# Four graph layers on one core: the norm's row product over 128 rows, the last graph's scores by two heads, and another order of every engine's list

## The chip, the core and the metric

One core of a Trainium2 chip runs one program. The metric is the device time of that program in microseconds (us). The core has five engines, each with an instruction queue of its own: TensorE (PE, products and transposes into PSUM), VectorE (DVE), ScalarE (ACT), GpSimd (POOL) and SyncE (SP, which here only issues DMAs). They are held together by semaphores that each instruction raises and waits for.

## What is computed

The input is `x` of 16 x 512 x 256 and `adj` of 16 x 512 x 512: 16 graphs of 512 nodes with 256 features. Four layers follow each other, each as `x = x + layer(relu(layernorm(x)), adj)`:

```
L0: xw = h @ W1.T; m = Be * (H.T @ xw); z = relu(Dn * (H @ m) + b1)     # H = adj != 0
    z = layer_norm(z) * gamma + beta; the same conv with W2, b2; + h
L1: e = leaky_relu(sj[j] + si[i] + ab); t = rows of adj * exp(e), divided by their sums
    relu(h @ Wk[0] + (t @ h) @ Wk[1] + (t @ t @ h) @ Wk[2] + bk)
L2: per head of 32 features: xp = h @ Wp + bp; xc = xp @ C.T
    att = tanh(adj * (xc @ xp.T)); relu(att @ xp)
L3: relu((adj @ h) @ kernel) * (row of h is not all zero)
```

## The kernel before

**Tiles.** A graph is four row tiles of 128 nodes. The weights stay in SBUF. Where float32 accuracy is wanted, an operand is split into a high part (type fp32r) and a low one, and a product is made of three: high by high, high by low, low by high (`three`, or two where one side is exact). The low parts come from DVE or POOL by a subtraction, the high ones mostly from ACT. PSUM is cut into three banks `ring_f`, handed round among the steps of layers 0 and 1, two double banks `ring_b` for the scores and the rest of layers 2 and 3, and `pv_acc`, in which the attends accumulate.

**Steps.** Each engine has a function of its own for each step, and one name on several engines is one step. Layers 0 and 1 are the f_ steps: `bn`, `variance`, `p_rstd` (POOL), `offset` and `f_h0` make a norm (k = 0 to 4 in their argument: H0, Z, H1, H2, H3); `f_H` and `f_HT` make the incidence matrix and its transpose from `adj_n` and `adj_t`, `f_dn` the node weights; then `f_m`, `f_u`, `f_conv1`, relu, `f_zT` (transposes), `f_stat`, `f_xw`, `f_m2`, `f_y`. In `f_hT`, `f_sj`, `f_q`, `f_max`, `f_mask`, `f_exp`, `f_sums`, `f_trans`, `f_tt`, `f_r1`, `f_r`, `f_x1` and `f_x2` the attention hop follows. Layers 2 and 3 are the k_ steps: `k_hT`, `k_xp`, `k_xc`, `k_xn`, then eight units (two halves of the heads by four row tiles). In each, PE makes four heads' scores in twelve 32-row products (`k_scores`, S0 to S7 below), DVE multiplies them by `at`, two heads at a time (`k_unit`, the gating), ACT takes tanh, two heads at a time, and PE multiplies with `xp_n` (`k_attend`, A0 to A7). `k_outT` transposes the result back and DVE adds it to `xb`; `k_ax` and `k_out` are layer 3; `k_y` on POOL adds the last sum before the store. `k_keep` and `k_xh` are copies on ACT.

**The row product.** The norm inside layer 0 is not applied to z itself. `xw` (line 1440) multiplies the raw z by the weights, and one product more adds the means and biases: `stat_t` rows 0 to 5 by `rowz` rows 0 to 5. It is the first of the group for each of four output tiles. `sel` by `rowb` does the like elsewhere, with 128 rows that are zero but for a few.

**Order.** Each engine's order is written out by hand as three lists: `first` (graphs 0 to 4), `turn` (a hardware loop) and `last`. `all_turns` (line 354) runs them; the loop goes from 5 to 15, so it has ten turns. An entry `(d, step, ...)` in `turn` is that step for the graph b - d: the engine works on graph b's layers 0 and 1 while it works on graph b-2's units and b-1's k_xp. In `first` the first number is the graph itself, in `last` it counts from the end (-1 is graph 15). Nothing but these lists and the semaphores sets what comes after what: an engine that waits holds back all that is behind in its list. SP's list (line 462) holds the loads (`next_adjt`, `next_adj`, `next_x`, ...) with the waits that say when their tile is free. `ends(g)` (line 191) is true for graph 15 in `last`, `apart(g)` for graph 14 there; these two use other banks for some steps, so that graph 14's `k_ax` and `k_out` may stand anywhere beside graph 15's scores.

**Waits that matter.** `k_scores` of unit u waits until both halves of unit u - 1 are gated (`gated`, line 1636), since it writes the same two banks; `k_attend` waits for both tanh of its unit. `f_m` 0 waits for all four low parts of h0, which POOL makes (`f_h0`, line 503). `k_xp` waits for the low part of `k_hT`. `k_outT` on DVE adds into `xb` and `k_outT` on PE waits for the copies `k_xh`. The last graph's `k_scores` 0 waits for its three inputs and for DVE's `k_outT` of graph 14.

## Time and profile before

| | |
|---|---|
| median of 3 runs | 1603.48 us (1602.44 to 1604.51) |
| the profiled execution | 1603.98 us, span 1602.0 us, mean granted clock 0.983 |
| PE busy | 1476.8 us, 92% |
| DVE busy | 1192.0 us, 74% |
| ACT busy | 886.4 us, 55% |
| POOL busy | 285.6 us, 18% |
| HBM traffic | 57 GB/s over the span |

How to read it: a share of busy time is an average over the fill at the start, twelve or so full turns and the tail. PE's busy time includes time at which one product waits for another inside PE, since the ends of its products are modelled. A granted clock of 1.00 is the upper of TensorE's two levels, 2.4 GHz. One row of the timeline can hold several instructions of one kind (x12), and the bracket at its end is the idle time before it, with the instruction that ended it.

### The profile page before, as it was taken

What the parts mean: (1) busy time and instruction counts of PE and PEld (TensorE: products, weight loads), DVE (VectorE), ACT (ScalarE), POOL (GpSimd) and SP (SyncE); (2) the same over time, 40 slices, a digit from 0 to 9 for tenths busy, and PEclk for the clock granted to TensorE, in tenths of its full rate; (3) what the DMA queues carried; (4) which work ended last, traced back from release to release, by engine and by line L of the source; (5) the groups of instructions that cost most, each with busy time, mean ns of one, the idle gap of its engine ahead of it and who ended that gap; (6) DMA issues with size and microseconds to landing.
All of it is one profiled execution on the core that took longest, in us unless ns stands there. A gap on an engine that the chain in (4) does not pass through costs nothing.

```text
span 1602.0 us, 28213 instructions
## 1 busy us (share of the span) xinstructions
PE 1476.8 (92%) x10426; PEld 1117.6 (70%) x10426; DVE 1192.0 (74%) x2667; ACT 886.4 (55%) x1501; POOL 285.6 (18%) x348
## 2 busy tenths in 40 slices
...
DMA packets 58554, 92.21 MB, mean 58 GB/s; under 512 B 4289, under 2 KB 23297, under 8 KB 58497
## 3 DMA queue, kind: packets, MB, share of 16 engines
...
## 4 chain that ended last, share of the span: by engine, by line
PE 65%; issue 16%; DVE 10%; ACT 5%; POOL 2%; DMA 1%; ACTq 0%; POOLq 0%; SPq 0%; DVEq 0%
PE ring_f L1360 41%; PE ring_b L1360 9%; PE ring_b L1640 6%; PE pv_acc L1656 6%; PE ring_f L1537 2%; POOL rstd L501 2%; ACT hf L580 1%; DVE att L1191 1%; DVE m L992 1%; ACT uz L570 1%; DVE bns L951 1%; DVE tr_l L992 1%; DVE uz L992 1%; PE ring_f L1437 1%; DVE rows L1119 1%
## 5 line engine op out<-in xcount | busy, mean ns | idle before, releaser
L1191 DVE TENSOR_TENSOR att<-ring_b,at 128x1024 f32<-128x1024 f32 x256 | 308.2, 1219 | 93.5 <-PE ring_b L1640 89.0
L728 ACT ACTIVATE att<-att 128x1024 f32<-128x1024 f32 x256 | 268.3, 1055 | 163.8 <-DVE att L1191 162.5
L501 POOL TENSOR_TENSOR rstd<-var,mhalf 128x4 f32<-128x4 f32 x80 | 81.7, 1021 | 735.4 <-DVE var L966 735.3
L1360 PE MATMUL ring_f<-w,uz 128*128 128x256 f32 (+1 forms) x896 | 197.0, 342 | 2.4 <-DVE uz L992 1.8
L1360 PE MATMUL ring_f<-m,tr_h 128*128 128x256 f32 x1024 | 190.8, 287 | 0.0
L1360 PEld LDWEIGHTS ring_f<-w,uz 128*128 128x128 f32 x896 | 150.7, 191 | 34.7 <-DVE uz L992 7.5
L1360 PEld LDWEIGHTS ring_f<-m,tr_h 128*128 128x128 f32 x1024 | 158.6, 191 | 22.8 <-issue 22.0
L1360 PEld LDWEIGHTS ring_f<-m,inc_n 128*128 128x128 f32 x1024 | 129.2, 197 | 37.0 <-issue 26.6
L1360 PE MATMUL ring_f<-m,inc_n 128*128 128x256 f32 x1024 | 136.3, 291 | 16.3 <-POOL m L505 16.2
L1360 PE MATMUL ring_f<-m,tr_l 128*128 128x256 f32 x512 | 144.5, 282 | 0.0
L1656 PE MATMUL pv_acc<-att,xp_n 128*32 128x512 f32 x1024 | 134.9, 604 | 4.6 <-ACT att L728 3.5
L1640 PE MATMUL ring_b<-xc_t,xp_s 32*128 32x512 f32 x1536 | 125.4, 427 | 13.0 <-ACT xp_n L570 5.6
L1360 PE MATMUL ring_b<-at,h 128*128 128x512 f32 x240 | 109.4, 600 | 5.8 <-ACT h L580 5.8
L575 ACT ACTIVATE m<-ring_f,be 128x256 fp32r<-128x256 f32 x128 | 53.7, 473 | 107.4 <-PE ring_f L1360 106.9
L1640 PEld LDWEIGHTS ring_b<-xc_t,xp_s 32*128 32x128 f32 x1536 | 64.4, 184 | 65.3 <-issue 34.7
L1360 PE MATMUL ring_f<-wk,uz 128*128 128x256 f32 x768 | 103.4, 284 | 0.0
L570 ACT ACTIVATE uz<-ring_f 128x512 fp32r<-128x512 f32 x128 | 71.6, 597 | 51.6 <-PE ring_f L1360 23.5
L1360 PEld LDWEIGHTS ring_f<-wk,uz 128*128 128x128 f32 x768 | 96.8, 190 | 2.5 <-issue 2.0
L1360 PEld LDWEIGHTS ring_f<-m,tr_l 128*128 128x128 f32 x512 | 97.9, 191 | 0.0
L520 POOL TENSOR_TENSOR h<-h,xb 128x256 f32<-128x256 f32 x64 | 47.4, 756 | 276.2 <-ACT h L756 276.2
L997 DVE SCALAR_TENSOR_TENSOR m<-ring_f,be,m 128x256 fp32r<-128x256 f32 x128 | 55.5, 477 | 43.1 <-ACT m L575 42.7
L505 POOL TENSOR_TENSOR m<-hf,m 128x256 fp32r<-128x256 f32 x64 | 53.0, 852 | 183.6 <-DVE m L1050 183.6
...
## 6 DMA issues: line engine op xcount, KB each, us to landing
...
```

The lines of the kernel that those rows point to most:

```text
L501: pool.tensor_tensor(rstd[k][:], var[k][:], mhalf[:], ALU.pow).then_inc(rstd_made[k].sem, 1)
L505: pool.tensor_tensor(m1[:, 1, i], hf[:, i], m1[:, 0, i].bitcast(F32), ALU.subtract).then_inc(h0_lo.sem, 1)
L520: pool.tensor_tensor(y_part[:, i], y_part[:, i], xb[:, i], ALU.add).then_inc(y_made.sem, 1)
L570: act.activation(dst, src, ACT.Copy).then_inc(made.sem, 1)
L575: ins = act.activation(dst_of(t), tile[:, i * D:(i + 1) * D], ACT.Copy, scale=by[:, t:t + 1])
L728: act.activation(v, v, ACT.Tanh).then_inc(tanh_made.sem, 1)
L992: dve.tensor_tensor(dst, src, hi.bitcast(F32), ALU.subtract).then_inc(made.sem, 1)
L997: ins = dve.scalar_tensor_tensor(dst_of(t), tile[:, i * D:(i + 1) * D], by[:, t:t + 1], hi_of(t).bitcast(F32), ALU.mult, ALU.subtract)
L1191: dve.tensor_tensor(att[:, u % 2, 2 * half:2 * half + 2], ring_b[half][:], at[:, u % NT].unsqueeze(1).broadcast_to([P, 2, N]), ALU.mult).t ...
L1360: ins = pe.matmul(dst, lhsT, rhs, start=(first and n == 0), stop=(last and n == len(pairs) - 1), skip_group_check=True)
L1640: ins = pe.matmul(ring_b[h // 2][:, h % 2], xp_s[head, p, part, t * P:(t + 1) * P], xc_t[head, c, part], start=(n == 0), stop=(n == 2), sk ...
L1656: ins = pe.matmul(pv_acc[h * KH:(h + 1) * KH, :], xp_n[:, t, ch:ch + KH], att[:, u % 2, h], start=(t == 0), stop=(t == NT - 1), skip_group ...
```

## The change

Four things change. `stat_t` and `rowz` are cleared whole in `set_up_w2` (two memsets more, and the counts SET_W2 and SET_DONE two higher), and `xw` then takes all 128 rows of both in its first product. For the last graph `k_scores` makes two heads at a time: three products for each of heads 0 and 1, behind the gating of the first half of the unit before, then the same for heads 2 and 3 behind the second half. All five engines have other lists for the loop. And `first` and `last` are other lists as well: `first` repeats the order of the loop from graph 1 on, and in `last` graph 14's `k_ax` and `k_out` stand ahead of the last graph's `k_scores` 0 on PE, ACT and DVE, and ACT's `k_keep` for the last graph moves from behind unit 7 into unit 3. The lists are shown for one loop turn: whole for POOL, SP and PE (old and new), the new one for DVE, and the head and the end of the new one for ACT; the old ones are in the code above. Of `last`, PE's end is shown, old and new.

```diff
@@ -340,7 +340,7 @@
-        SET_W1, SET_COLUMNS, SET_W2, SET_DONE = 1, 12, 24, 42
+        SET_W1, SET_COLUMNS, SET_W2, SET_DONE = 1, 12, 26, 44
@@ -461,21 +461,21 @@
             def turn(b):
                 run_turn(b, G, (
-                    (0, next_x), (2, next_at), (4, store), (3, next_at2), (0, next_adj), (0, next_wrow),
+                    (0, next_x), (3, next_at2), (0, next_wrow), (2, next_at), (4, store), (0, next_adj),
                     (0, next_adjt),
                 ))
 
...
@@ -521,27 +521,27 @@
             def turn(b):
                 run_turn(b, G, (
-                    (0, p_rstd, 0), (0, f_h0, 0), (0, f_h0, 1), (3, k_y, 1), (3, k_y, 2), (0, f_h0, 2),
-                    (0, f_h0, 3), (3, k_y, 3), (0, f_sum, 0), (1, p_rstd, 3), (0, f_sum, 1), (0, f_sum, 2),
-                    (0, f_sum, 3), (0, p_rstd, 1), (0, p_rstd, 2), (2, p_rstd, 4), (2, k_y, 0),
+                    (0, p_rstd, 0), (0, f_h0, 0), (3, k_y, 1), (3, k_y, 2), (3, k_y, 3), (0, f_h0, 1),
+                    (0, f_h0, 2), (0, f_h0, 3), (0, f_sum, 0), (0, f_sum, 1), (0, f_sum, 2), (0, f_sum, 3),
+                    (1, p_rstd, 3), (0, p_rstd, 1), (0, p_rstd, 2), (2, p_rstd, 4), (2, k_y, 0),
                 ))
...
@@ -759,19 +759,19 @@
+                    (0, f_h0, 0), (2, k_unit, 2, 0), (1, f_r, 1), (0, f_h0, 1), (0, f_h0, 2), (2, k_unit, 2, 1),
+                    (0, f_h0, 3), (2, k_unit, 3, 0), (2, k_keep), (2, k_unit, 3, 1), (0, f_m, 0), (0, f_m, 1),
+                    (2, k_xh, 0), (2, k_unit, 4, 0), (0, f_u, 0), (0, f_u, 1), (0, f_relu, 0), (2, k_unit, 4, 1),
+                    (0, f_relu, 1), (2, k_unit, 5, 0), (0, f_relu, 2), (0, f_relu, 3), (0, f_zT, 0), (0, f_zT, 1),
+                    (0, f_zT, 2), (1, k_h2, 0), (1, k_h2, 1), (0, f_zT, 3), (2, k_unit, 5, 1), (1, k_h2, 2),
+                    (1, k_h2, 3), (0, f_stat), (2, k_unit, 6, 0), (0, f_xw, 0), (0, f_xw, 1), (2, k_unit, 6, 1),
...
+                    (2, k_out, 1), (0, f_tt, 0), (0, f_tt, 1), (0, f_tt, 2), (0, f_tt, 3), (1, k_unit, 0, 0),
+                    (1, k_unit, 0, 1), (0, f_r, 0), (1, k_unit, 1, 0), (1, k_unit, 1, 1),
...
@@ -900,7 +899,9 @@
                 step(dve.memset(sel[:].bitcast(F32), 0.0))
-                step(dve.memset(rowb[:].bitcast(F32), 0.0), now=True)
+                step(dve.memset(rowb[:].bitcast(F32), 0.0))
+                step(dve.memset(stat_t[:].bitcast(F32), 0.0))
+                step(dve.memset(rowz[:].bitcast(F32), 0.0), now=True)
@@ -1211,145 +1212,144 @@
+                    (0, bn, 0, 0), (3, bn, 4, 2), (3, bn, 4, 3), (3, variance, 4), (3, offset, 4), (1, f_hT, 0),
+                    (1, f_hT, 1), (0, bn, 0, 1), (2, k_xc), (1, f_q, 0), (1, f_q, 1), (0, bn, 0, 2), (1, f_max, 0),
+                    (1, f_mask, 0), (3, k_mask), (1, f_q, 2), (1, f_max, 1), (1, f_q, 3), (1, f_mask, 1),
+                    (1, f_max, 2), (3, k_ax, 0), (1, f_mask, 2), (1, f_max, 3), (1, f_mask, 3), (3, k_ax, 1),
+                    (2, k_split, 0), (1, f_sums), (1, f_trans, 0), (1, f_trans, 1), (1, f_trans, 2),
+                    (1, f_trans, 3), (2, k_split, 1), (1, f_tt, 0), (1, f_tt, 1), (0, bn, 0, 3), (1, f_tt, 2),
+                    (1, f_tt, 3), (2, k_unit, 0, 0), (2, k_unit, 0, 1), (0, f_HT, 0), (2, k_unit, 1, 0),
+                    (0, variance, 0), (0, f_HT, 1), (2, k_unit, 1, 1), (1, f_r, 0), (0, f_HT, 2), (0, offset, 0),
+                    (0, f_HT, 3), (2, k_unit, 2, 0), (2, k_unit, 2, 1), (1, f_r, 1), (0, f_H), (0, f_be),
+                    (2, k_unit, 3, 0), (0, f_h0), (0, f_dn, 0), (2, k_unit, 3, 1), (0, f_dn, 1), (2, k_unit, 4, 0),
+                    (2, k_unit, 4, 1), (1, f_x2, 0), (1, f_x2, 1), (0, f_dn, 2), (0, f_dn, 3), (1, bn, 3, 0),
+                    (1, bn, 3, 1), (0, f_m, 0), (1, bn, 3, 2), (0, f_m, 1), (0, f_dn2), (1, bn, 3, 3),
+                    (1, variance, 3), (0, f_u, 0), (0, f_u, 1), (2, k_unit, 5, 0), (0, f_conv1, 0),
+                    (0, f_conv1, 1), (2, k_unit, 5, 1), (0, f_conv1, 2), (0, f_conv1, 3), (0, bn, 1, 0),
+                    (0, bn, 1, 1), (1, offset, 3), (0, bn, 1, 2), (0, f_zT, 0), (0, f_zT, 1), (0, bn, 1, 3),
+                    (0, f_zT, 2), (0, variance, 1), (0, f_zT, 3), (0, f_stat), (2, k_unit, 6, 0),
+                    (2, k_unit, 6, 1), (0, f_xw, 0), (2, k_unit, 7, 0), (0, f_xw, 1), (2, k_unit, 7, 1),
+                    (0, f_m2, 0), (0, f_m2, 1), (1, k_hT), (2, k_outT, 0), (2, k_outT, 1), (0, f_y, 0),
+                    (0, f_y, 1), (0, bn, 2, 0), (0, bn, 2, 1), (0, bn, 2, 2), (0, bn, 2, 3), (0, variance, 2),
+                    (2, bn, 4, 0), (2, bn, 4, 1), (0, offset, 2),
...
@@ -1440,7 +1440,7 @@
                 zh, zl = (a[:].rearrange("p a n -> p (a n)") for a in (uz, m2))
                 for i in (2 * q, 2 * q + 1):
-                    pairs = [(stat_t[0:6, i * P:(i + 1) * P], rowz[0:6])] if ks[-1] == HT_ - 1 else []
+                    pairs = [(stat_t[:, i * P:(i + 1) * P], rowz[:])] if ks[-1] == HT_ - 1 else []
@@ -1632,15 +1632,18 @@
-                else:
+                elif not ends(g):
                     pe.wait_ge(gated.sem, gated.after(g, 2 * u))
-                for n, (p, c) in enumerate(((0, 0), (0, 1), (1, 0))):
-                    for h in range(4):
-                        head = slice(h * KH, (h + 1) * KH)
-                        ins = pe.matmul(ring_b[h // 2][:, h % 2], xp_s[head, p, part, t * P:(t + 1) * P],
-                                        xc_t[head, c, part], start=(n == 0), stop=(n == 2), skip_group_check=True)
-                        if n == 2 and h % 2 == 1:
-                            ins.then_inc(scored.sem, 1)
+                for heads in (((0, 1), (2, 3)) if ends(g) else ((0, 1, 2, 3),)):
+                    if ends(g) and u > 0:
+                        pe.wait_ge(gated.sem, gated.after(g, 2 * u - 1 + heads[0] // 2))
+                    for n, (p, c) in enumerate(((0, 0), (0, 1), (1, 0))):
+                        for h in heads:
+                            head = slice(h * KH, (h + 1) * KH)
+                            ins = pe.matmul(ring_b[h // 2][:, h % 2], xp_s[head, p, part, t * P:(t + 1) * P],
+                                            xc_t[head, c, part], start=(n == 0), stop=(n == 2), skip_group_check=True)
+                            if n == 2 and h % 2 == 1:
+                                ins.then_inc(scored.sem, 1)
@@ -1698,18 +1701,18 @@
-                    (0, f_m, 0), (2, k_scores, 3), (1, f_x2, 1), (2, k_attend, 2), (0, f_m, 1), (2, k_scores, 4),
-                    (0, f_u, 0), (2, k_attend, 3), (0, f_u, 1), (2, k_scores, 5), (0, f_conv1, 0), (0, f_conv1, 1),
-                    (0, f_conv1, 2), (0, f_conv1, 3), (2, k_attend, 4), (2, k_scores, 6), (0, f_zT, 0),
-                    (0, f_zT, 1), (2, k_attend, 5), (0, f_zT, 2), (0, f_zT, 3), (0, f_xw, 0), (0, f_xw, 1),
-                    (0, f_stat), (2, k_scores, 7), (0, f_xw, 2), (0, f_xw, 3), (2, k_attend, 6), (0, f_m2, 0),
-                    (0, f_m2, 1), (1, k_hT), (2, k_outT, 0), (0, f_y, 0), (2, k_attend, 7), (0, f_y, 1),
-                    (2, k_outT, 1), (1, k_xp, 0), (1, k_xp, 1), (1, k_xc, 0), (1, k_xc, 1), (1, k_xn, 0),
-                    (0, f_hT, 0), (0, f_hT, 1), (1, k_xn, 1), (0, f_sj), (0, f_q, 0), (0, f_q, 1), (2, k_ax, 0, 0),
-                    (0, f_q, 2), (0, f_q, 3), (2, k_ax, 0, 1), (2, k_ax, 1, 0), (2, k_ax, 1, 1), (2, k_out, 0),
-                    (2, k_out, 1), (0, f_tt, 0), (0, f_tt, 1), (0, f_tt, 2), (1, k_scores, 0), (0, f_tt, 3),
-                    (0, f_r1), (0, f_r, 0), (1, k_scores, 1), (0, f_r, 1), (0, f_x1), (1, k_attend, 0),
-                    (1, k_scores, 2), (1, k_attend, 1), (0, f_x2, 0),
+                    (0, f_m, 0), (0, f_m, 1), (2, k_attend, 3), (0, f_u, 0), (0, f_u, 1), (2, k_scores, 5),
+                    (0, f_conv1, 0), (0, f_conv1, 1), (0, f_conv1, 2), (0, f_conv1, 3), (2, k_attend, 4),
+                    (0, f_zT, 0), (0, f_zT, 1), (2, k_scores, 6), (0, f_zT, 2), (0, f_zT, 3), (0, f_xw, 0),
+                    (0, f_xw, 1), (0, f_stat), (2, k_attend, 5), (0, f_xw, 2), (2, k_scores, 7), (0, f_xw, 3),
+                    (0, f_m2, 0), (1, k_hT), (0, f_m2, 1), (2, k_attend, 6), (2, k_attend, 7), (0, f_y, 0),
+                    (2, k_outT, 0), (2, k_outT, 1), (0, f_y, 1), (1, k_xp, 0), (1, k_xp, 1), (1, k_xc, 0),
+                    (1, k_xc, 1), (1, k_xn, 0), (1, k_xn, 1), (0, f_hT, 0), (0, f_hT, 1), (0, f_sj), (0, f_q, 0),
+                    (0, f_q, 1), (2, k_ax, 0, 0), (0, f_q, 2), (0, f_q, 3), (2, k_ax, 0, 1), (2, k_ax, 1, 0),
+                    (2, k_ax, 1, 1), (2, k_out, 0), (2, k_out, 1), (0, f_tt, 0), (0, f_tt, 1), (0, f_tt, 2),
+                    (1, k_scores, 0), (0, f_tt, 3), (0, f_r1), (0, f_r, 0), (1, k_scores, 1), (0, f_r, 1),
+                    (1, k_attend, 0), (1, k_scores, 2), (0, f_x1), (1, k_attend, 1), (1, k_scores, 3),
+                    (0, f_x2, 0), (1, k_attend, 2), (1, k_scores, 4), (0, f_x2, 1),
...
-                (-2, k_attend, 6), (-2, k_attend, 7), (-2, k_outT, 0), (-2, k_outT, 1), (-1, k_xp, 0),
-                (-1, k_xp, 1), (-1, k_xc, 0), (-1, k_xc, 1), (-1, k_xn, 0), (-1, k_xn, 1), (-1, k_scores, 0),
-                (-2, k_ax, 0, 0), (-1, k_scores, 1), (-2, k_ax, 0, 1), (-1, k_attend, 0), (-1, k_scores, 2),
-                (-2, k_ax, 1, 0), (-1, k_attend, 1), (-1, k_scores, 3), (-2, k_ax, 1, 1), (-1, k_attend, 2),
-                (-1, k_scores, 4), (-1, k_attend, 3), (-1, k_scores, 5), (-2, k_out, 0), (-1, k_attend, 4),
-                (-1, k_scores, 6), (-2, k_out, 1), (-1, k_attend, 5), (-1, k_scores, 7), (-1, k_attend, 6),
-                (-1, k_attend, 7), (-1, k_outT, 0), (-1, k_outT, 1), (-1, k_ax, 0, 0), (-1, k_ax, 0, 1),
...
+                (-2, k_outT, 1), (-1, k_xp, 0), (-1, k_xp, 1), (-1, k_xc, 0), (-1, k_xc, 1), (-1, k_xn, 0),
+                (-1, k_xn, 1), (-2, k_ax, 0, 0), (-2, k_ax, 0, 1), (-2, k_ax, 1, 0), (-2, k_ax, 1, 1),
+                (-2, k_out, 0), (-2, k_out, 1), (-1, k_scores, 0), (-1, k_scores, 1), (-1, k_attend, 0),
+                (-1, k_scores, 2), (-1, k_attend, 1), (-1, k_scores, 3), (-1, k_attend, 2), (-1, k_scores, 4),
+                (-1, k_attend, 3), (-1, k_scores, 5), (-1, k_attend, 4), (-1, k_scores, 6), (-1, k_attend, 5),
+                (-1, k_scores, 7), (-1, k_attend, 6), (-1, k_attend, 7), (-1, k_outT, 0), (-1, k_outT, 1),
+                (-1, k_ax, 0, 0), (-1, k_ax, 0, 1), (-1, k_ax, 1, 0), (-1, k_ax, 1, 1), (-1, k_out, 0),
+                (-1, k_out, 1),
             )
```

## Rows read from the trace of the kernel before

**Rows 1.** the profile's page, part 1: busy time, share of the span, instructions
```profile
PE 1476.8 (92%) x10426; PEld 1117.6 (70%) x10426; DVE 1192.0 (74%) x2667; ACT 886.4 (55%) x1501; POOL 285.6 (18%) x348
```

**Rows 2.** one turn: stretch, us, PE, PEld, DVE, ACT, POOL busy, PEclk, DMA, GB/s
```profile
670.00:764.00 94.00, 90.64 (x652) 68.56 (x651) 72.70 (x165) 54.66 (x94) 17.60 (x21) 1.00 0.18 59
```

**Rows 3.** PE timeline, f_m 0 of graphs 2, 5, 8: start, us, operation
```profile
199.67 3.52 PE L1360 MATMUL ring_f<-m,inc_n 128*128 128x256 f32 x28
...
481.65 2.08 PE L1360 MATMUL ring_f<-m,inc_n 128*128 128x256 f32 x16
...
764.07 2.08 PE L1360 MATMUL ring_f<-m,inc_n 128*128 128x256 f32 x16
```

**Rows 4.** waits of PE from 670 to 764: who waits <- for whom
```profile
PE ring_b L1360 <- DVE tr_l L992: 1.4, 1, 1.4
```

**Rows 5.** PE timeline around k_xp and f_sj of that turn
```profile
716.78 0.60 PE L1664 MATMUL ring_b<-ident,xh_t 128*128 128x128 f32 x4
718.58 3.06 PE L1360 MATMUL ring_b<-tr_l,wp 128*128 128x512 f32 x12 [1.20 <-DVE xb L1199]
...
726.21 1.63 PE L1360 MATMUL ring_f<-uz,v 128*128 128x512 f32 x6 [0.63 <-DVE uz L992]
```

**Rows 6.** PE timeline, scores and ax in the last graph's stretch
```profile
1544.71 0.98 PE L1640 MATMUL ring_b<-xc_t,xp_s 32*128 32x512 f32 x12 [1.56 <-DVE xc_t L992]
1545.68 1.95 PE L1360 MATMUL ring_f<-at,h 128*128 128x512 f32 x4
...
1566.64 0.98 PE L1640 MATMUL ring_b<-xc_t,xp_s 32*128 32x512 f32 x12
...
1570.14 0.98 PE L1640 MATMUL ring_b<-xc_t,xp_s 32*128 32x512 f32 x12
```

**Rows 7.** DVE timeline, gating of the last graph's unit 7
```profile
1571.21 2.36 DVE L1191 TENSOR_TENSOR att<-ring_b,at 128x1024 f32<-128x1024 f32 x2 [1.14 <-PE ring_b L1640]
```

**Rows 8.** PE timeline, row products and the change from scores to products
```profile
702.95 0.38 PE L1360 MATMUL ring_f<-rowz,stat_t 6*128 6x256 f32 x1
...
703.82 0.38 PE L1360 MATMUL ring_f<-rowz,stat_t 6*128 6x256 f32 x1
...
750.94 0.97 PE L1640 MATMUL ring_b<-xc_t,xp_s 32*128 32x512 f32 x12
751.84 0.50 PE L1360 MATMUL ring_f<-m,tr_h 128*128 128x256 f32 x2
...
754.81 0.28 PE L1360 MATMUL ring_f<-rowb,sel 128*128 128x256 f32 x1
...
755.64 0.28 PE L1360 MATMUL ring_f<-rowb,sel 128*128 128x256 f32 x1
```

**Rows 9.** DVE timeline, k_outT 1 and a bn of H3 behind f_y
```profile
717.84 0.68 DVE L1199 SCALAR_TENSOR_TENSOR xb<-ring_b,xb 128x512 f32<-128x512 f32 x1
...
719.75 0.41 DVE L951 BATCH_NORM_STATS2 bns<-xb 128x6 f32<-128x256 f32 x1
```

**Rows 10.** PE timeline, transposes of f_zT
```profile
787.60 1.09 PE L1437 MATMUL ring_f<-ident,rows 128*128 128x128 f32 x8
```

**Rows 11.** ACT timeline, the last relus of that turn
```profile
786.22 1.37 ACT L618 ACTIVATE rows<-rows 128x512 f32<-128x512 f32 x2
```

**Rows 12.** SP timeline: the load of adjT; then its time to landing
```profile
745.09 0.37 SPq L375 DMA_DIRECT2D rows<-in_adjT  x1
...
DMA to landing us min/median/max: 5.9/6.1/6.4
```

**Rows 13.** POOL timeline, an addition in graph 0 and two f_h0 in the loop
```profile
16.05 1.17 POOL L514 TENSOR_TENSOR xf<-x_in,hf 128x256 f32<-128x256 f32 x1
...
757.92 1.80 POOL L505 TENSOR_TENSOR m<-hf,m 128x256 fp32r<-128x256 f32 x2 [9.78 <-DVE m L1050]
```

**Rows 14.** groups by line, the set-up: busy us, mean ns, idle before
```profile
L903 DVE MEMSET rowb<- 128x256 f32 x1 | 0.3, 272 | 0.0
```

**Rows 15.** ACT timeline, ACT's xc copy of the last graph
```profile
1542.38 1.03 ACT L570 ACTIVATE xc_t<-ring_b 128x1024 fp32r<-128x1024 f32 x1 [1.27 <-PE ring_b L1360]
```

More of the change, by code:

```diff
@@ L1308, in _ @@
[L1308 to L1311 removed]
+                (0, bn, 0, 0), (0, bn, 0, 1), (0, bn, 0, 2), (0, bn, 0, 3), (0, f_HT, 0), (0, variance, 0),
@@ new lines, in _ @@
+                (0, f_HT, 1), (0, f_HT, 2), (0, offset, 0), (0, f_HT, 3), (0, f_H), (0, f_be), (0, f_h0),
+                (0, f_dn, 0), (0, f_dn, 1), (0, f_dn, 2), (0, f_dn, 3), (0, f_m, 0), (0, f_m, 1), (0, f_dn2),
+                (0, f_u, 0), (0, f_u, 1), (0, f_conv1, 0), (0, f_conv1, 1), (0, f_conv1, 2), (0, f_conv1, 3),
+                (0, bn, 1, 0), (0, bn, 1, 1), (0, bn, 1, 2), (0, f_zT, 0), (0, f_zT, 1), (0, bn, 1, 3),
+                (0, f_zT, 2), (0, variance, 1), (0, f_zT, 3), (0, f_stat), (0, f_xw, 0), (0, f_xw, 1),
@@ L1312, in _ @@
+                (4, f_xw, 1), (2, k_unit, 7, 1), (4, f_m2, 0), (4, f_m2, 1), (3, k_hT), (2, k_outT, 0),
+                (2, k_outT, 1), (4, f_y, 0), (4, f_y, 1), (4, bn, 2, 0), (4, bn, 2, 1), (4, bn, 2, 2),
+                (4, bn, 2, 3), (4, variance, 2), (2, bn, 4, 0), (2, bn, 4, 1), (4, offset, 2),
             )
             last = (
[L1314 to L1315 removed]
```

527 lines of the change are left out of this document (243 added, 284 removed).

## The prediction

> **What bounds the kernel now.** I read the page first. TensorE (PE) is busy for 92% of the span [rows 1], so a reordering alone can win at most what PE does not use. The stretch view of one loop turn then says where the rest is not: of 94 us PE is busy 90.64, at full granted clock, with VectorE (DVE) at 72.70 and ScalarE (ACT) at 54.66 [rows 2]. A turn lasts 94.14 us: f_m 0 of graph 5 starts at 481.65 and that of graph 8 at 764.07, three turns later [rows 3]. The waits of that turn name one large one, 1.4 us in front of k_out for the low part of k_ax [rows 4]; two smaller ones stand in the timeline, 1.20 before k_xp and 0.63 before f_sj [rows 5]. So steady turns are PE-bound, and what counts in them is PE's own time, first, and those gaps, second. At the end of the kernel, where only the last graph is left, PE waits and DVE's gating products with ACT's tanh set the pace [rows 6, 7].
>
> **PE time of the row product.** In xw, each of four output tiles has one 6-row product and three full ones. From one such product to the next the timeline shows 0.87 us (702.95 to 703.82). The 128-row product on `sel` and `rowb`, same columns, with six full products, takes 0.83 us for seven (754.81 to 755.64), 0.119 each [rows 8]. Four of those would be 0.48. So the time lost is not in the product itself but at the change between 6 and 128 rows, on both sides. A change between scores (32-row tiles) and full products shows the same kind of price: scores start at 750.94, the next full product at 751.84, and it is drawn longer than its neighbours [rows 8]. Three of the four products save 0.39 (1.17 together), the first, which follows something that changes tiling anyway, about 0.1: 1.25 us a graph. It lies on PE, hence on the path. In graph 0 ACT's set-up copies end later than xw, so I count nothing there; 15 graphs have it. The zeros need no work per graph: rows 6 to 127 of stat_t are cleared once, and 128 rows are read at the same 0.119.
> The Trainium skill, page "TensorEngine Tiling (Array Packing)", section Tiling Modes, Key Properties, says that changing the tiling mode drains TensorE; the rows above agree. The same skill, page "TensorE: Matmul & The Clock Gate", section "Why this matters for your kernels", says that a single K=32 product takes the time of a K=128 one, which would leave nothing to win here; that is the fourth rival.
>
> **The loop's new PE order.** Before, 8 score units and 8 attends stand between full products in 13 groups (S3, A2, S4, A3, S5, A4+S6, A5, S7, A6, A7, S0, S1, A0+S2+A1); after, in 12. By the rows at 750.94 and 751.84 a group costs about 0.2 beside its products: 0.2 less.
> k_outT 1 moves from behind f_y 1 to before it. The 1.20 us wait for DVE's xb before k_xp [rows 5] then ends under f_y 1. What is late next is the norm: f_y on DVE, four bn, variance, rstd on POOL, offset, four f_h1, f_hT, uz, f_sj. DVE no longer has k_outT (0.60) and one bn of H3 (0.33) in it [rows 9], so f_sj starts 8.5 us after f_y 1 ends, where it is 9.5 now (716.74 to 726.21); PE has 6.5 us of work there, with k_outT 1's 0.37 now before. That is 0.6 less wait in total.
> f_zT 0 now comes right behind A4 instead of behind A4 and S6. Its last transpose needs the fourth relu. Now the transposes start at 787.60 [rows 10] just when the relus that begin at 786.22 end (787.59) [rows 11]. In the new order conv 3 is ahead of the first bn on DVE, which gains some 0.3; PE is there 0.9 earlier: 0.25 more wait.
> f_m2 0 loses A6 as cover and gets S7 and f_xw 3 behind f_xw 2 (2.0 us), while ACT's and DVE's two operations each take 2.0: nothing. k_out's 1.4 stays: k_ax 1 is now behind f_mask 3 on DVE, but exp 3 ends at about 736.2, and max and mask (0.6 and 0.7) end at 738.2, when ACT's copy is there.
> S3, S4, A2 and x2 1 go to the end of the turn. S2 needs both halves of unit 1, for which DVE has f_HT, variance and f_HT between; r_0 and r_1 cover this within 0.1. f_HT 0, now behind unit 0, waits for adjT: issued at 745.1, landing in 6.1 (5.9 to 6.4) [rows 12], thus at 751.2, before S1's scores are there (751.95), and DVE idles then in either case. POOL has k_y 1 to 3 between f_h0 0 and f_h0 1: seven operations of 0.72 to 0.9 [rows 13] from 764.1 end at 769.5, f_m 0 starts at 770.2. Here and for DVE's dn beside POOL I allow 0.3 in all.
> A turn: -1.25 - 0.2 - 0.6 + 0.25 + 0.3 = **-1.5 us**. Bounds: -2.0 (no new wait) and -0.5 (one more wait of 1 us). The first turns from graph 2 on and the last one have the same order, so it counts 3 + 10 + 1 = 14 times: -21.0.
>
> **First turns.** f_m 0 goes from 199.67 (graph 2) to 481.65 (graph 5), 281.98 us, against 282.42 for three loop turns [rows 3]; but at 199.67 S0 to S4 and A0 to A2 are already issued, at 481.65 only S0 to S2 and A0, A1. Less those (3 units and their groups, 3.3 us) the old turns are 2.9 worse than loop turns; the new ones repeat the loop: -2.9. Graph 1's turn: the row product's 1.25, but f_m2 0 then waits for xw's low part with only f_xw 3 as cover, and ax of ACT and DVE bound f_tt as before: -1.1. Start: f_HT 0 stands before variance and waits for adjT, but f_h0 on POOL is bound by inc_n's load: 0.3 later. Two memsets in set_up_w2: that of rowb (128x256) is 272 ns [rows 14], so 0.27 and, for twice the columns, 0.27 to 0.54; one bn leaves the same stretch: 0.2. Together +0.5.
>
> **The tail.** Now ax and out of graph 14 stand between the last graph's scores, where PE would wait for DVE (S6 to S7: 1566.64 to 1570.14, 3.5 us; S0 at 1544.71) [rows 6]. After, all 16 ax products and 48 out products come before S0, and ax waits for xn_made: ACT's xc copy (1542.38) [rows 15], two h3 and two xn copies, with 0.4 that S7's later place costs: 1545.65. ax is 6.85 (four take 1.9 with the edges), then 1.4 for the low part, then 3.0: S0 starts at 1556.95, 12.2 later than now. Two heads at a time let S(u+1)'s first half run while DVE gates the second half of unit u. The loop is then: two gating operations 2.36 [rows 7], tanh 1.1, attend 1.0, first half of scores 1.0 with latency: 5.5 us for two units, 2.75 each. The half of the scores is not in the trace; it lies between half of 0.97 and the 1.07 that the first half takes now, giving 2.55 to 2.85; DVE alone would give 2.36, today's coupling 3.5. Seven steps: 19.25, and 0.9 to the first gating: unit 7 is gated from 1577.1, where now it is 1571.21 [rows 7]: +5.9. k_keep (1.0 on ACT) moves from behind tanh 7 into unit 3: +0.8. Sum +6.7, bounds +3.1 and +12. What follows (A7, k_outT, norm, ax, out) is unchanged.
>
> **Sum.** The profiled execution took 1603.98 us, span 1602.0; the median shown is 1603.48, so the two stand together. 1603.98 - 21.0 - 1.1 - 2.9 + 0.5 + 6.7 = 1586.2; I say **1586**.
>
> **Rivals.** (1) Smoother than I walk it: no new waits (-2.0 a turn, 7 more) and a tail at 2.36 without k_keep's cost (3.6 less): 1575. For it: DVE idles 21 us a turn. 0.17. (2) The new order costs one more wait of about 1 us a turn, 14 in all: 1600. For it: four places above have under 0.3 us of slack. 0.14. (3) Slower than before: f_m 0's wait for f_h0's low part. It is behind three k_y on POOL, which run beside DVE's dn; in graph 0 such POOL operations took 1.17 instead of 0.74 [rows 13]. Seven at 1.17 end at 772.3, 2.1 late, and 29 in all: 1615; it decides from 1.5 us a turn. Against it: beside DVE's two-input work the two at 757.92 took 0.9. 0.09. (4) The row product gives nothing, since its rows are free and the 0.87 belongs to the accumulation into xw: 1586 + 18.8 = 1605. Against it is the row at 754.81, also accumulating. 0.05. (5) Two heads do not shorten the loop, because A(u) holds back S(u+2) and the half takes as long as the whole: 3.5 a unit, 5.2 more: 1591. 0.07. My forecast has 0.48.
>
> **Range and chances.** Its own cases give 1579 to 1594. The range takes in (1), (5) and (2): 1574 to 1604. About 0.2% (3.2 us) is what a measurement can tell from no change. Faster: 0.48 + 0.17 + 0.07 and half of (2) = 0.79. Same: half of (2) and most of (4) = 0.10. Slower: 0.11.
>
> **What would show it.** rowz products at 0.12 from their neighbours and 0.48 between them. f_m 0 to f_m 0 in 92.6. No wait of k_xp for xb, about 1 to 2 us of PE idle before f_sj; 0.25 before the fourth transpose of f_zT 0. Last graph: S0 near 1557 less some 18, then 2.75 a unit. Wrong if PE waits for POOL's m at f_m 0, for adjT through unit 1, or if the rowz spacing stays.

## The result, and the profile after

The changed kernel takes 1600.72 us (median of 20 runs, 1594.83 to 1604.26) against 1603.63 (20 runs, 1602.44 to 1606.78). The ratio is 0.9976, with a 95% interval of 0.9969 to 0.9984. It is 2.9 us faster where 17.4 were forecast. The interval excludes no change, but the gain is smaller than the 3.2 us that the prediction took as what can be told apart. The runs spread over 9.4 us where those of before spread over 4.3. The profiled execution has a span of 1597.7 us. Its page, part 1, and the granted clock in 40 slices (answering to [rows 1]):

```profile
PE 1469.8 (92%) x10426; PEld 1120.5 (70%) x10426; DVE 1216.2 (76%) x2669; ACT 882.7 (55%) x1501; POOL 307.3 (19%) x348
...
PEclk9899899999999999999999999999999999999998
```

**Turns.** f_m 0 of graphs 5 to 15 starts at 477.58, 571.93, 664.74, 757.56, 851.88, 944.70, 1037.46, 1131.77, 1224.54, 1317.34 and 1410.10: seven turns of 92.8 us and three of 94.3. The stretch view (columns as in [rows 2]) tells two neighbours apart by one thing only, the clock:

```profile
664.74:757.56 92.82, 89.47 (x652) 68.60 (x651) 75.19 (x165) 54.59 (x93) 18.79 (x21) 1.00 0.19 59
757.56:851.88 94.32, 90.98 (x653) 69.98 (x651) 75.18 (x165) 54.72 (x93) 18.79 (x21) 0.98 0.18 58
```

The PE timeline of both says where. f_sj (`uz,v`) starts 48.8 us into the turn in either, behind the same wait; in the second it and f_q 0 behind it take 1.5 us more:

```profile
713.57 1.63 PE L1360 MATMUL ring_f<-uz,v 128*128 128x512 f32 x6 [1.25 <-DVE uz L993]
715.04 1.61 PE L1360 MATMUL ring_f<-wq,uz 128*128 128x258 f32 x12
...
806.38 2.25 PE L1360 MATMUL ring_f<-uz,v 128*128 128x512 f32 x6 [1.24 <-DVE uz L993]
808.43 2.55 PE L1360 MATMUL ring_f<-wq,uz 128*128 128x258 f32 x12
```

```profile
713.50:718.00 4.50, 4.43 (x23) 3.44 (x23) 3.25 (x8) 4.50 (x11) 0.00 (x0) 1.00 0.00 0
805.00:808.50 3.50, 2.26 (x9) 1.73 (x8) 2.87 (x5) 3.50 (x8) 0.41 (x1) 0.81 0.00 0
808.50:813.00 4.50, 4.50 (x21) 3.54 (x20) 1.80 (x7) 3.25 (x9) 0.00 (x0) 0.77 0.00 0
```

A stretch at 0.77 is one that spends part of its time at the lower level, 1.2 GHz. The timeline has five such f_sj, of 2.2 to 2.7 us in place of 1.63: those of graphs 3, 5, 8, 11 and 15. Below, such a stretch is called a drop. PE's waits in the turn from 664.74 (answering to [rows 4]) show that the wait for xb is gone, and that a sum not much smaller stands elsewhere (1.20 + 0.63 before, 1.25 + 0.33 now):

```profile
PE ring_b L1360 <- DVE tr_l L993: 1.4, 1, 1.4
PE ring_f L1360 <- DVE uz L993: 1.3, 1, 1.3
PE ring_f L1504 <- ACT hf L580: 0.3, 2, 0.2
PE ring_f L1537 <- DVE tr_l L993: 0.2, 1, 0.2
PE ring_f L1437 <- ACT rows L618: 0.2, 1, 0.2
```

**The last graph** (PE timeline; [rows 6] is the same stretch of before). k_xp starts at 1521.57, 15.7 us earlier than before (1537.31), and the end comes only 4.3 us earlier:

```profile
1521.57 3.06 PE L1360 MATMUL ring_f<-tr_l,wp 128*128 128x512 f32 x12
...
1529.70 8.80 PE L1360 MATMUL ring_f<-at,h 128*128 128x512 f32 x16 [2.29 <-ACT xp_n L570]
1539.91 3.07 PE L1360 MATMUL ring_f<-k,tr_l 128*128 128x256 f32 x24 [1.41 <-DVE tr_l L993]
1542.91 0.98 PE L1643 MATMUL ring_b<-xc_t,xp_s 32*128 32x512 f32 x12
...
1561.23 1.73 PE L1659 MATMUL pv_acc<-att,xp_n 128*32 128x512 f32 x8 [1.41 <-ACT att L728]
1562.89 1.67 PE L1643 MATMUL ring_b<-xc_t,xp_s 32*128 32x512 f32 x12
...
1565.93 0.97 PE L1643 MATMUL ring_b<-xc_t,xp_s 32*128 32x512 f32 x6 [0.20 <-DVE att L1192]
...
1570.50 1.06 PE L1659 MATMUL pv_acc<-att,xp_n 128*32 128x512 f32 x8 [1.29 <-ACT att L728]
```

The eight products of one attend take 1.06 at 1570.50 and 1.73 at 1561.23. In the stretch view the clock of this part, from k_xp to the last scores, is 1.00 before and falls again and again after (first row before, the others after; the first of the after rows lies ahead of k_xp, among graph 14's units):

```profile
1550.00:1560.00 10.00, 10.00 (x66) 3.32 (x66) 6.99 (x7) 6.47 (x7) 0.00 (x0) 1.00 0.02 3
```

```profile
1512.00:1517.00 5.00, 4.85 (x27) 2.44 (x28) 2.97 (x4) 2.98 (x5) 0.00 (x0) 0.50 0.00 0
...
1529.70:1538.50 8.80, 8.80 (x16) 3.50 (x16) 0.86 (x2) 1.50 (x5) 0.00 (x0) 0.81 0.00 0
...
1561.00:1565.00 4.00, 3.77 (x24) 1.22 (x28) 1.27 (x2) 2.06 (x3) 0.00 (x0) 0.57 0.00 0
```

So there are two questions: what the tail costs, and what the clock costs.

### The profile page after: what moved, and what is told of

Same layout as the page of the kernel before. It is cut to its first block, busy times and chain, and to the rows that moved or that the text cites. A ratio compares the mean times of both kernels' runs of the same rounds, so it can differ in the third digit from the quotient of the medians.

```text
span 1597.7 us, 28235 instructions
## 1 busy us (share of the span) xinstructions
PE 1469.8 (92%) x10426; PEld 1120.5 (70%) x10426; DVE 1216.2 (76%) x2669; ACT 882.7 (55%) x1501; POOL 307.3 (19%) x348
## 4 chain that ended last, share of the span: by engine, by line
PE 61%; issue 18%; DVE 10%; ACT 7%; POOL 3%; DMA 0%; ACTq 0%; POOLq 0%; DVEq 0%; SPq 0%
PE ring_f L1360 40%; PE ring_b L1360 9%; PE ring_b L1643 5%; PE pv_acc L1659 5%; POOL rstd L501 2%; ACT rows L618 2%; DVE m L993 1%; DVE bns L952 1%; DVE tr_l L993 1%; ACT att L728 1%; PE ring_f L1537 1%; DVE att L1192 1%; PE ring_f L1437 1%; DVE rows L1071 1%; DVE uz L993 1%
## 5 line engine op out<-in xcount | busy, mean ns | idle before, releaser
L1360 PE MATMUL ring_f<-w,uz 128*128 128x256 f32 (+1 forms) x896 | 189.4, 333 | 1.5 <-DVE uz L993 0.9
L1643 PE MATMUL ring_b<-xc_t,xp_s 32*128 32x512 f32 x1536 | 130.9, 434 | 2.6 <-DVE att L1192 2.5
L520 POOL TENSOR_TENSOR h<-h,xb 128x256 f32<-128x256 f32 x64 | 63.3, 1011 | 270.7 <-ACT h L756 270.7
L570 ACT ACTIVATE m<-ring_f 128x256 fp32r<-128x256 f32 (+1 forms) x96 | 43.5, 454 | 79.0 <-PE ring_f L1360 78.4
```

The lines of the kernel that those rows point to most:

```text
L520: pool.tensor_tensor(y_part[:, i], y_part[:, i], xb[:, i], ALU.add).then_inc(y_made.sem, 1)
L570: act.activation(dst, src, ACT.Copy).then_inc(made.sem, 1)
L1360: ins = pe.matmul(dst, lhsT, rhs, start=(first and n == 0), stop=(last and n == len(pairs) - 1), skip_group_check=True)
L1643: ins = pe.matmul(ring_b[h // 2][:, h % 2], xp_s[head, p, part, t * P:(t + 1) * P], xc_t[head, c, part], start=(n == 0), stop=(n == 2), sk ...
```

## The experiments

Each was timed beside the kernel before; the times of before were 1603.5 to 1603.9 in all four groups. Names with a_ start from the changed kernel (1600.7), names with b_ from the kernel before. In brackets stand the ratio to the kernel before and its 95% interval.

**The tail.** `a_tail_old4`: the old end of PE's, ACT's and DVE's lists (with k_keep and k_xh 0 of ACT where they were), four heads at a time. PE's part:

```diff
-                (-1, k_xn, 1), (-2, k_ax, 0, 0), (-2, k_ax, 0, 1), (-2, k_ax, 1, 0), (-2, k_ax, 1, 1),
-                (-2, k_out, 0), (-2, k_out, 1), (-1, k_scores, 0), (-1, k_scores, 1), (-1, k_attend, 0),
+                (-1, k_xn, 0), (-1, k_xn, 1), (-1, k_scores, 0), (-2, k_ax, 0, 0), (-1, k_scores, 1),
+                (-2, k_ax, 0, 1), (-1, k_attend, 0), (-1, k_scores, 2), (-2, k_ax, 1, 0), (-1, k_attend, 1),
...
```

> The changed kernel, with the tail of the kernel before: from k_xp 0 of the last graph on PE, from k_hT of the last graph on ACT and DVE, the old order (k_ax and k_out of graph 14 between the last graph's scores), and four heads at a time in k_scores. Everything ahead of that is the changed kernel. Theory A (the tail lost the gain: ax and out stand ahead of S0, and a half of the scores takes as long as the whole): k_xp to the end takes 64.7 us as in the kernel before in place of 76.1, so 1600.7 - 11.4 = 1589. Theory B (the tail's loss sits ahead of k_xp, in graph 14's units, and the clock is what costs behind it; only the low-clock stretches come back): 1596 to 1598.

Measured: 1588.54 (0.9899, 0.9885 to 0.9914). Theory A, to half a microsecond. k_xp starts at 1520.99 and the span is 1586.5, so 65.5 us lie between, where the changed kernel has 76.1. Its trace has five drops at f_sj too, so the 12.2 us are the tail's.

`a_four` undoes the two heads alone, `a_tail_old2` the order alone:

```diff
-                elif not ends(g):
+                else:
                     pe.wait_ge(gated.sem, gated.after(g, 2 * u))
-                for heads in (((0, 1), (2, 3)) if ends(g) else ((0, 1, 2, 3),)):
-                    if ends(g) and u > 0:
-                        pe.wait_ge(gated.sem, gated.after(g, 2 * u - 1 + heads[0] // 2))
...
```

> The changed kernel with four heads at a time in the last graph's k_scores, waiting for both gated halves as before; all orders are the new ones. Theory A: the unit takes 3.5 us at the full clock in place of the 3.29 measured with two heads, 7 x 0.21 = 1.5 more: 1602. Theory B (two heads only cost: the halves fill PE with 1.0 us more a unit and bring nothing, as DVE could have gated at the same pace): 1597 or less.

> The old order of the tail, but two heads at a time in the last graph's k_scores. Theory A (a half takes 0.96 us, as long as the whole): PE has 1.1 us more in each of seven units, in a stretch (S0 to S7) where it idles 2.1 us in all in the kernel before: 5 to 6 us more than with four heads in the same order, about 1595. Theory B (the half-wise wait lets the scores start sooner and the 1.1 us lies beside DVE's gating): no more than four heads, 1587 to 1589.

Measured: a_four 1605.12 (1.0006, 0.9997 to 1.0014), a_tail_old2 1588.87 (0.9903, 0.9889 to 0.9918). In the new order two heads are worth 4.4 us by the medians, three times what theory A gave, and close to the 5.2 of the prediction's fifth rival; in the one trace of a_four a unit takes 3.68 us (S0 1542.07, S7 1567.86, clock 0.80) in place of 3.29. In the old order they are worth nothing, and cost nothing. Theory A was wrong about a half: it is drawn as long as the whole (0.96) only where PE stands between the halves. Where both gatings are done, the twelve products run as one (timeline of a_tail_old2):

```profile
1547.68 0.96 PE L1640 MATMUL ring_b<-xc_t,xp_s 32*128 32x512 f32 x6 [0.37 <-DVE att L1191]
1548.81 0.96 PE L1640 MATMUL ring_b<-xc_t,xp_s 32*128 32x512 f32 x6 [0.17 <-DVE att L1191]
...
1552.30 0.98 PE L1640 MATMUL ring_b<-xc_t,xp_s 32*128 32x512 f32 x12
```

**The row product.** `b_row128` puts it into the kernel before, `a_row6` takes it out of the changed one:

```diff
-                    pairs = [(stat_t[0:6, i * P:(i + 1) * P], rowz[0:6])] if ks[-1] == HT_ - 1 else []
+                    pairs = [(stat_t[:, i * P:(i + 1) * P], rowz[:])] if ks[-1] == HT_ - 1 else []
```

> The kernel before with the row product over 128 rows (and its two memsets), nothing else. Theory A (its time lies on PE in the old order as well): 1603.85 - 15 x 1.25 = 1585, turns of 92.9. Theory B (part of it comes back as wait, since DVE and ACT then are behind PE at k_xp and f_sj, or as low clock): 1590 to 1597, with turns of 94.4 among those of 92.9.

> The changed kernel with 6 rows of stat_t and rowz again in xw's first product. Theory A (the time is lost at the change between 6 and 128 rows, on both sides; but S7 stands between the two pairs now, so two of the four products follow a change of tiling anyway): 2 x 0.39 + 2 x 0.1 = 1.0 a graph for 15 graphs, 1600.7 + 15 = 1616. Theory B (four full prices of 0.39, whatever stands before): 1624. Theory C (rows are free): 1600.7.

Measured: b_row128 1583.44 (0.9871, 0.9857 to 0.9885), 20.1 us less by this edit alone, and 17.3 below the whole change. This is theory A. Every loop turn takes 92.90, where it was 94.14: 1.24 a turn, and PE's three waits are those of before to 0.1. The spacing forecast at 0.48 is there:

```profile
692.88 0.28 PE L1362 MATMUL ring_f<-rowz,stat_t 128*128 128x256 f32 x1
...
693.35 0.29 PE L1362 MATMUL ring_f<-rowz,stat_t 128*128 128x256 f32 x1
...
693.83 0.28 PE L1362 MATMUL ring_f<-rowz,stat_t 128*128 128x256 f32 x1
```

a_row6 takes 1615.01 (1.0069, 1.0055 to 1.0083), 14.3 more than the changed kernel, close to theory A. Its undisturbed turns are 93.7, so the edit is worth 0.9 there, since S7 now parts the four products into two pairs. First a_row6, then the changed kernel:

```profile
981.69 0.38 PE L1360 MATMUL ring_f<-rowz,stat_t 6*128 6x256 f32 x1
...
982.54 0.38 PE L1360 MATMUL ring_f<-rowz,stat_t 6*128 6x256 f32 x1
...
983.39 0.98 PE L1643 MATMUL ring_b<-xc_t,xp_s 32*128 32x512 f32 x12
984.20 0.27 PE L1360 MATMUL ring_f<-rowz,stat_t 6*128 6x256 f32 x1
...
984.95 0.38 PE L1360 MATMUL ring_f<-rowz,stat_t 6*128 6x256 f32 x1
```

```profile
690.25 0.39 PE L1360 MATMUL ring_f<-rowz,stat_t 128*128 128x256 f32 x1
...
690.84 0.28 PE L1360 MATMUL ring_f<-rowz,stat_t 128*128 128x256 f32 x1
```

From A5, which stands ahead of the first of them, to f_m2 it is 5.04 us in a_row6 (980.69 to 985.73) and 4.08 in the changed kernel (689.26 to 693.34). The 14.3 us are not the row product alone: six of the ten loop turns in the trace of a_row6 are long (95.2 to 95.3), where the changed kernel has three.

**The order of the loop and of the first turns.** `a_row6_tail4`: a_row6 with the old tail.

> The new order of the loop and of the first turns alone: the changed kernel with the 6-row product, and the old tail with four heads. If the parts add up: 1588.5 + 14.3 = 1602.8, so the new order is worth 1 us against the kernel before, where the prediction had 0.25 us a turn and 2.9 at the start, 6 to 7 us. Rival (the row product and the order share a gain, PE's idle time ahead of f_sj): clearly off that sum, 1598 or less, or 1607 or more.

Measured: 1606.11 (1.0006, 0.9996 to 1.0015; runs from 1600.6 to 1607.9). Without the row product and the tail, the new order is 2.6 us slower by the medians, which is within the noise of no change, and neither side of the expectation was met clearly. Its loop turns are 93.7 (seven) or 95.2 (three). So at the full clock the order does save, 0.4 a turn against 94.14, and the long turns take it back. With 128 rows it saves 0.1 (92.8 against the 92.90 of b_row128). The sum of the parts is off by 3, as much as two long turns.

**The clock.** `a_fill` adds work that nobody uses, `a_xn1` moves one step, both to shorten the wait ahead of f_sj:

```diff
+            def f_fill(g):
+                for i in range(2 * NT):
+                    pe.transpose(pv_acc[:, (i % NT) * P:(i % NT + 1) * P], ident[:], ident[:])
...
-                    (1, k_xc, 1), (1, k_xn, 0), (1, k_xn, 1), (0, f_hT, 0), (0, f_hT, 1), (0, f_sj), (0, f_q, 0),
+                    (1, k_xc, 1), (1, k_xn, 0), (1, k_xn, 1), (0, f_hT, 0), (0, f_hT, 1), (0, f_fill), (0, f_sj),
```

```diff
-                    (1, k_xc, 1), (1, k_xn, 0), (1, k_xn, 1), (0, f_hT, 0), (0, f_hT, 1), (0, f_sj), (0, f_q, 0),
+                    (1, k_xc, 1), (1, k_xn, 0), (0, f_hT, 0), (0, f_hT, 1), (1, k_xn, 1), (0, f_sj), (0, f_q, 0),
```

> The changed kernel with eight useless transposes of the identity into pv_acc between f_hT 1 and f_sj (graphs 2 to 15), where PE idles 1.25 us. They take some 0.8 us there. Their result is overwritten and nothing else changes. Theory A (the 1.5 us that every third turn costs is the lower clock granted behind this idle time): the gap is 0.45, no turn of 94.3 is left, and f_sj's own low stretch in the last graph goes: four or five times 1.5 less, 1594 to 1595. Theory B (the slow turns come from something periodic that only shows there, as loads or the loop's own code): the slow turns stay, 1601; if the transposes push f_sj back it is more.

> The changed kernel with PE's k_xn 1 behind f_hT 1 instead of ahead of f_hT 0, in all turns. PE idles as long in all, but in smaller pieces: the wait ahead of f_sj falls from 1.25 to 0.83 and the rest comes ahead of f_hT. Theory A (what brings the clock down is one long gap): the slow turns go, 1594. Theory B (what counts is PE's idle time in the whole stretch): every third turn stays at 94.3, 1600 to 1601.

Measured: a_fill 1593.22 (0.9932, 0.9919 to 0.9945), a_xn1 1592.09 (0.9928, 0.9915 to 0.9941). 112 useless transposes make the kernel 7.5 us faster. None of the ten loop turns of either is long (92.7 to 92.9), and no f_sj behind graph 0 is drawn longer than 1.65; five drops of 1.5 are the 7.5 us. The five runs of each spread over 1.9 and 2.3 us where the 20 of the changed kernel spread over 9.4. The timeline of a_fill, in the place of the row at 806.38 above:

```profile
802.67 1.04 PE L1509 MATMUL pv_acc<-ident 128*128 128x128 f32 x8
804.09 1.63 PE L1360 MATMUL ring_f<-uz,v 128*128 128x512 f32 x6 [0.37 <-DVE uz L993]
```

Theory A in both: in a_fill f_sj starts when DVE lets it, as in the changed kernel, and what differs is only what PE did before.

`a_outT` undoes the move to which the prediction gave 0.6 us, PE's k_outT 1 ahead of f_y 1:

```diff
-                    (2, k_outT, 0), (2, k_outT, 1), (0, f_y, 1), (1, k_xp, 0), (1, k_xp, 1), (1, k_xc, 0),
+                    (2, k_outT, 0), (0, f_y, 1), (2, k_outT, 1), (1, k_xp, 0), (1, k_xp, 1), (1, k_xc, 0),
```

> The changed kernel with PE's k_outT 1 behind f_y 1 again in all turns. The prediction gave this move 0.6 us a turn. Theory A (it does save, but it also makes the one long gap ahead of f_sj that costs the clock): turns of 93.1 to 93.4 and no slow one among them, so about the mean of now, 93.25: 1599 to 1603, with less spread from run to run. Theory B (it saves nothing, since the norm bounds f_sj either way): turns of 92.8, none slow: 1593 to 1594.

Measured: 1630.74 (1.0154, 1.0141 to 1.0167): neither theory. Nine of the ten loop turns take 95.65, 2.85 above 92.8. 1.5 of it is the clock. The other 1.3 is there without a drop too, since the first loop turn, all at 1.00, takes 94.12: 0.8 of it is a new wait ahead of k_xp, and PE is busy for 0.4 more (89.85 in place of 89.47).

```profile
713.84 3.06 PE L1360 MATMUL ring_b<-tr_l,wp 128*128 128x512 f32 x12 [0.78 <-DVE xb L1200]
...
722.95 2.49 PE L1360 MATMUL ring_f<-uz,v 128*128 128x512 f32 x6 [1.25 <-DVE uz L993]
725.23 2.31 PE L1360 MATMUL ring_f<-wq,uz 128*128 128x258 f32 x12
```

The wait ahead of f_sj is 1.25 as in the changed kernel. A second one of 0.78, 9 us before it, goes with a drop in nearly every turn where there was one in three. No run separates this wait from the rest that the edit changes, such as the length of the turn.

The length of a wait does not tell by itself. The longest wait of each turn, 1.41 ahead of k_out, has the full clock behind it (changed kernel, timeline and stretch view):

```profile
726.37 3.07 PE L1360 MATMUL ring_b<-k,tr_l 128*128 128x256 f32 x24 [1.41 <-DVE tr_l L993]
```

```profile
726.37:731.37 5.00, 5.00 (x48) 4.64 (x48) 3.99 (x9) 2.66 (x7) 1.59 (x1) 1.00 0.20 31
```

And the kernel before and b_row128 have 1.20, 0.63 and 1.41 in every loop turn, with a clock of 1.00 in all ten. So a_fill and a_xn1 show that the drop hangs on what PE does ahead of f_sj; why there, and why in one turn of three, stays open.

**The clock in the tail.** `a_xn1_warm` puts `f_fill` steps into a_xn1's last list (16 transposes ahead of graph 14's k_ax, 4 behind each of A0 to A6), `b_row128_warm` puts one of 40 behind the last k_outT of b_row128.

> a_xn1 (new tail order, two heads) with useless transposes in PE's idle time of the last graph: 16 into pv_acc ahead of graph 14's k_ax, 4 into ring_f1 behind each attend A0 to A6. Nothing else changes. Theory A (what the tail is longer than forecast by is the low clock: ax 8.8 in place of 6.85 and 3.3 a unit in place of 2.75): S0 comes 1.5 to 2 earlier and S0 to S7 takes 19.5 to 20.5 in place of 23.6: 1592.1 - 5 = 1587. Theory B (the unit is 3.3 for another reason, a wait of ACT or DVE in the loop of two heads; the four transposes a unit then cost as much as they give): 1590 to 1593.

> b_row128 with 40 useless transposes into ring_f1 behind the last k_outT, where PE idles 5.75 us ahead of the last graph's k_ax and the granted clock in the k_ax behind it is about 0.8. Theory A (the idle time brings the clock down): the 16 products take 7.0 to 7.3 in place of 8.7 to 9.3, 1583.4 - 1.9 = 1581.5. Theory B (the clock there does not depend on them): 1583.4, or more if the transposes hold up k_ax.

Measured: a_xn1_warm 1590.43 (0.992, 0.9908 to 0.9933), b_row128_warm 1580.77 (0.9857, 0.9843 to 0.9872). The second is theory A, and 2.2 of its 2.7 us stand in the 16 products of the last k_ax, first in b_row128, then with the fill:

```profile
1562.23:1571.50 9.27, 9.27 (x16) 3.72 (x16) 0.86 (x2) 1.62 (x5) 0.00 (x0) 0.76 0.00 0
```

```profile
1560.84:1567.95 7.11, 7.11 (x16) 2.93 (x16) 0.86 (x2) 1.62 (x5) 0.00 (x0) 1.00 0.00 0
```

The first is theory A for k_ax and theory B for the units: from k_xp to S0 19.8 us in place of 21.3, from S0 to S7 23.4 in place of 23.6. So 1.5 us of the tail is clock ahead of S0. From S3 to S7 (1543.10 to 1556.26) a_xn1_warm is at the full clock, and four units, each with 0.6 us of transposes, still take 3.29 each:

```profile
1543.10:1556.26 13.16, 11.35 (x97) 5.03 (x97) 9.41 (x9) 9.66 (x11) 0.00 (x0) 1.00 0.00 1
```

The unit's 3.3 has another cause as well. ACT's timeline of a_xn1 offered one:

```profile
1547.37 1.04 ACT L570 ACTIVATE xb<-xa 128x1024 f32<-128x1024 f32 x1
1548.32 1.04 ACT L728 ACTIVATE att<-att 128x1024 f32<-128x1024 f32 x1
1550.60 0.60 ACT L570 ACTIVATE xh_t<-pv_acc 128x512 f32<-128x512 f32 x1 [1.25 <-PE pv_acc L1659]
1551.10 3.89 ACT L728 ACTIVATE att<-att 128x1024 f32<-128x1024 f32 x4
```

k_keep (`xb<-xa`) stands in the middle of unit 3, and k_xh 0 waits for A3 with tanh 4 behind it. `a_xn1_act` puts both back:

```diff
-                (-1, k_unit, 1, 1), (-1, k_unit, 2, 0), (-1, k_unit, 2, 1), (-1, k_unit, 3, 0), (-1, k_keep),
-                (-1, k_unit, 3, 1), (-1, k_xh, 0), (-1, k_unit, 4, 0), (-1, k_unit, 4, 1), (-1, k_unit, 5, 0),
+                (-1, k_unit, 3, 1), (-1, k_unit, 4, 0), (-1, k_xh, 0), (-1, k_unit, 4, 1), (-1, k_unit, 5, 0),
...
+                (-1, k_keep), (-1, k_xh, 1), (-1, k_h3, 0), (-1, k_h3, 1), (-1, k_h3, 2), (-1, k_h3, 3),
```

> a_xn1 (new tail order, two heads) with two copies of ACT's last list back where the kernel before has them: k_keep behind unit 7 instead of inside unit 3, and k_xh 0 between the halves of unit 4 instead of ahead of both. In the trace of a_xn1 ACT stands 1.25 us at k_xh 0, waiting for PE's fourth attend, while the first half of unit 4 is gated already. Theory A (the unit's 3.3 us is partly ACT's list): k_keep's 1.0 and the 1.25 both lie on the loop, S0 to S7 takes 21.5 in place of 23.6: 1590. Theory B (DVE, PE and the low clock set the loop and ACT catches up): 1592, S0 to S7 23.6.

Measured: 1592.34 (0.9933, 0.9919 to 0.9946; 1589.50 to 1594.33). In the profiled execution S0 to S7 takes 21.5 us, as theory A had it, and that execution took 1589.50; but the median is no lower than a_xn1's. The lists do hold up the loop in the one trace there is; that it makes the kernel faster is not shown.

**Together.** `a_xn1_tail4` is a_xn1 with the old tail, `a_xn1_tail4_warm` adds the 40 transposes.

> Both finds together: the changed kernel with k_xn 1 behind f_hT 1, and the old tail with four heads. If they are independent: 1592.1 (a_xn1) less the 12.2 of a_tail_old4 against the changed kernel = 1580, below the 1583.4 of the kernel before with the row product alone. If part of the 12.2 was the clock of graph 14's units, which a_xn1 has back already (its 1512 to 1517 is at full clock), 10.6 to 11: 1581.5. Rival: no better than b_row128, 1583 to 1584, since the new order of the loop is worth nothing.

> a_xn1_tail4 with 40 useless transposes into ring_f1 behind the last k_outT. In b_row128 they took the last k_ax from 9.3 to 7.1 us and the time from 1583.4 to 1580.8. The same here if it is the clock of that one stretch: 1580.8 - 1.7 to 2.6 = 1578.5. Rival: nothing left to gain, 1580.8.

Measured: 1580.80 (0.9857, 0.9843 to 0.9872) and 1580.93 (0.985, 0.9835 to 0.9865; 1577.73 to 1581.47). The first is as expected and beats both kernels, by 23 and by 20 us. The second is no better by the median, though its last k_ax took 7.10: its profiled execution has two turns of 94.3 and 94.4, with a wait of 0.81 ahead of f_sj. So the order of a_xn1 makes the drop rarer (two turns of fifty in five traces) and doesn't rule it out. The kernel before with the row product and the fill, 1580.77, is as fast.

## Why the prediction was wrong

The forecast was 1586, the result 1600.7. Two steps failed: the sum has no term for TensorE's clock, which cost 7.5 us, and the tail was priced at 6.7 where it costs 12.2. Its steps in turn:

- **What bounds the loop** (PE, and the gaps): right. **The row product** (-1.25 a graph): right, 1.24 in the order it was read from. In the new order it is 0.9, since S7 parts the four products; the step "three of the four save 0.39" was not redone for the new order. The other steps of the order made up for most of it: with 6 rows they save 0.4 a turn (94.14 to 93.7) where their terms add up to 0.25.
- **k_outT 1 and f_sj** (-0.6): nearly right for the stretch, wrong for the waits. The sentence "f_sj starts 8.5 us after f_y 1 ends" held (702.85 + 2.15 to 713.57 is 8.6, where it was 9.5). Less k_outT 1's 0.37, which stands ahead of f_y 1 now, that is 0.5 saved. But PE's waits from k_xp to f_sj fell only from 1.20 + 0.63 [rows 5] to 1.25 + 0.33, since two waits of 0.16 for `hf` came ahead of f_hT. Undone in the new order (a_outT) the move is worth 1.3 at the full clock. The wait at f_zT (0.25 forecast) is 0.17.
- **A turn**: 92.8 at full clock where 92.6 was forecast. What failed is that I took the clock of [rows 2], 1.00, for a constant of the loop, and gave it no term, without a reason. Two waits of 1.20 and 0.63, 8 us apart, were turned into one of 1.25 and two of 0.16; the first pair never cost the clock in the loop turns of before, the second did in three of the ten of this execution, and in five f_sj of the whole kernel, at 1.5 us each. a_fill and a_xn1 price it: 7.5 and 8.6 us. This is the larger part of what the order lost: forecast at 6 us of gain with the first turns, measured at 2.6 of loss by the medians (a_row6_tail4), which is not clear of no change.
- **The tail** (+6.7): right in kind, 12.2 in size (a_tail_old4). From k_xp to S0 it is 21.3 us, where the prediction's own figures give 19.6 (1556.95 less 1537.31): k_ax takes 8.80 in place of 6.85, which is the clock (0.81; a_xn1_warm gave back 1.5). A unit takes 3.29 in place of 2.75, 3.8 in seven units. There the rows at 1561.23 and 1562.89 are drawn at a low clock, but a_xn1_warm takes 3.29 at 1.00 too; the two copies in ACT's list hold it up by 2.0 from S0 to S7 in the one trace of a_xn1_act (clock 0.84, in a_xn1 0.80). I priced k_keep at 0.8 and did not see k_xh 0, which had moved ahead of both halves of unit 4. How the 3.8 splits stays open.
- **Together**: 7.5 for the clock at f_sj, 5.5 for the tail and 14 x 0.16 for the turns are 15.2, where 14.7 were missed.
- **Rivals.** (1) did not come: there are new waits, and a unit takes 3.29. (2), one more wait a turn, came out at the right time, 1600, by another mechanism: PE's waits in a turn grew by 0.1 in all, and what grew was the work behind one of them. That the result lies inside the stated range is luck, since this rival alone had widened it so far. (3), POOL, did not happen: f_m 0 waits for nothing. (4) fell with b_row128. (5): two heads bring 4.4 in this order (a_four).

The Trainium skill, page "TensorE: Matmul & The Clock Gate", section "Part 1: The HAM clock gate", says that the clock depends on how busy TensorE has been. The rows of a_fill and b_row128_warm agree: only PE's work ahead of the stretch was changed, and f_sj went from 2.25 back to 1.63 us in the one, the granted clock of k_ax from 0.76 to 1.00 in the other. The prediction cites that page for another point and leaves this one out.
